# The readout of the last state moved behind the rates and the second drive in each step of a selective scan (one Trainium2 core)

## The reference, cut to what matters

```
def step(h, inp):
    d_t, u_t, B_t, C_t = inp
    dA = jnp.exp(d_t[..., None] * A)
    dBu = (d_t * u_t)[..., None] * B_t[:, None, :]
    h = dA * h + dBu
    y = jnp.einsum('bdn,bn->bd', h, C_t)
    return (h, y)
```

## Time and profile before

| what | value |
|---|---|
| median of 3 runs | 1948.91 us (1948.72 to 1953.33) |
| the profiled execution's own time | 1953.92 us |
| its span, first to last instruction | 1952.1 us |
| mean granted TensorE clock, share of full | 0.916 |
| PE busy over the span | 1711.4 us (88%) |
| state loop, from the first readout's start to the last's | 463.6 to 1043.0 us |

### The profile page before, as it was taken

One profiled execution on the slowest core, in us unless ns is written; L12 is line 12 of the kernel. 1 busy time (PEld: TensorE's weight loads), 2 busy tenths in 40 slices (PEclk: granted clock), 3 DMA queues, 4 the chain that ended last, 5 costly groups with the idle time before them and its releaser, 6 DMA issues.

```text
span 1952.1 us, 24426 instructions
## 1 busy us (share of the span) xinstructions
PE 1711.4 (88%) x9096; PEld 821.3 (42%) x9096; DVE 1011.8 (52%) x1520; ACT 761.7 (39%) x1201; POOL 703.1 (36%) x430
## 2 busy tenths in 40 slices
PE   7888886898999999999997759999812979899998
PEld 4666663542322332332333525444401557644443
DVE  2444444255888888888884333222359464522121
ACT  1333332196676666666661222111413240112121
POOL 0433330215998998998995010000000014000000
PEclk8999997798999999999999768999865879789999
DMA  2111101002000100100100600111062100101110
GB/s 68 32 32 32 32 27 52 0 8 96 12 12 7 29 12 7 29 12 7 29 6 17 223 1 0 33 48 32 5 143 70 33 0 1 44 1 43 44 43 21
DMA packets 36491, 65.63 MB, mean 34 GB/s; under 512 B 13509, under 2 KB 22617, under 8 KB 34981
## 3 DMA queue, kind: packets, MB, share of 16 engines
q1 hardware_dynamic: 33204, 63.42, 11.0%
q10 hardware_dynamic: 3200, 1.07, 0.2%
HBM read 55.80 MB, written 8.67 MB: 33 GB/s over the span
## 4 chain that ended last, share of the span: by engine, by line
PE 80%; DVE 12%; ACT 2%; DMA 2%; issue 2%; POOL 1%; SPq 1%; DVEq 0%; ACTq 0%; POOLq 0%
PE ps L845 17%; PE ps L888 7%; PE ps L1376 6%; PE ps L2123 6%; PE ps L2112 6%; PE ps L860 5%; PE ps L201 4%; PE ps L1389 3%; PE ps L342 3%; PE ps L347 3%; PE ps L224 3%; PE ps L360 2%; DVE arena L477 2%; PE ps L1887 2%; PE ps L1903 2%
## 5 line engine op out<-in xcount | busy, mean ns | idle before, releaser
L1156 POOL TENSOR_TENSOR arena<-arena 128x768 f32<-128x768 f32 x248 | 521.5, 2122 | 75.2 <-DVE arena L1106 45.0
L845 PE MATMUL ps<-arena 32*128 32x512 f32 x2016 | 368.7, 647 | 2.9 <-DMA arena<-m_bd 2.9
L1106 DVE TENSOR_TENSOR arena<-arena,ps 128x1024 f32<-128x1024 f32 x248 | 302.0, 1218 | 11.7 <-POOL arena L1156 5.5
L845 PEld LDWEIGHTS ps<-arena 32*128 32x128 f32 x2016 | 130.0, 184 | 194.2 <-issue 165.2
L1086 DVE TENSOR_TENSOR arena<-arena,ps 128x1024 f32<-128x1024 f32 x124 | 151.4, 1221 | 87.5 <-PE ps L845 87.5
L1012 ACT ACTIVATE arena<-arena 128x1024 f32<-128x1024 f32 x124 | 131.0, 1057 | 166.1 <-DVE arena L1086 166.1
L2069 POOL TENSOR_TENSOR arena<-arena 128x1024 f32<-128x1024 f32 x16 | 29.9, 1896 | 435.0 <-DVE arena L2002 421.7
L888 PE MATMUL ps<-arena 128*32 128x512 f32 (+15 forms) x1024 | 136.2, 604 | 9.4 <-DVE arena L1106 8.9
L1019 ACT ACTIVATE arena<-ps 128x1024 f32<-128x1024 f32 x124 | 127.0, 1024 | 19.7 <-PE ps L845 3.4
L1021 ACT ACTIVATE arena<-arena 128x1024 f32<-128x1024 f32 x124 | 131.1, 1057 | 3.9
L1376 PE MATMUL ps<-arena 128*128 128x512 f32 x288 | 131.8, 602 | 0.6 <-ACT arena L1441 0.6
(11 more groups left out here) (291 smaller groups left out, 2345.3 us busy)
## 6 DMA issues: line engine op xcount, KB each, us to landing
arena<-ctxT SPq DMA_DIRECT2D x32, 257.0 KB, 3.0
arena<-ctxT SPq DMA_DIRECT2D x8, 1028.0 KB, 15.2
arena<-L_ffn_w SPq DMA_DIRECT2D x16, 512.0 KB, 4.3
arena<-ctx_rows SPq DMA_DIRECT2D x8, 960.0 KB
m_rows<-arena SPq DMA_DIRECT2D x16, 256.0 KB, 3.0
arena<-m_rows SPq DMA_DIRECT2D x64, 64.0 KB
arena<-L_ffn_eW SPq DMA_DIRECT2D x8, 512.0 KB, 3.5
m_yd<-arena SPq DMA_DIRECT2D x64, 32.0 KB, 2.3
```

Source lines behind the costliest of these rows:

```text
L845: mm = nc.tensor.matmul(ps[:, bank + jj, :], weights[r], m_row[r, n // CH % 2, n % CH, :], start=start, stop=True)
L1106: nc.vector.tensor_tensor(m_h[:, u, n % 2], m_xa[:, u, n % 2], ps[:, bank:bank + 2, :], ALU.add).then_inc(S["m_use"], 1)
L1156: nc.gpsimd.tensor_tensor(x, x, m_h[:, u, (n - 1) % 2].rearrange("p j d -> p (j d)")[:, own], ALU.mult).then_inc(S["m_kept"], 1)
```

## The change

In each step of PE's program the call of `read_out(n - 1)` moves from between the drive of unit 0 and the rates to behind the drive of unit 1, ahead of the logs. The ring's order, all semaphores and the programs of all other engines stay as they are.

```diff
             logs(1)
             for n in range(STEPS):
                 drive(n, 0)
-                if n:
-                    read_out(n - 1)
                 if rated(n + 2):
                     rates(n + 2)
                 drive(n, 1)
+                if n:
+                    read_out(n - 1)
                 if rated(n + 2):
                     logs(n + 2)
             read_out(STEPS - 1)
```

## The result

The changed kernel takes 2003.24 us (median of 4 runs, 1996.8 to 2008.46) against 1948.90 before: the ratio is 1.0272, 95% interval 1.0238 to 1.0305. The forecast was 2001 us, slower. The profiled execution took 2003.58 us against 1953.92. From the first readout to the last the loop now takes 464.0 to 1091.7, 627.7 us, against 579.4: 48.3 of the 49.7 us between the two profiled executions.

A forecast was written before the change was run, and what follows sets the result against it. The prediction took a 4.57 us chain through readout, rates, DVE and unit 1's state as the bound, replaced by 5.05 through the logs. 120 x 0.48 = 57.6, less 5.6, on 1948.9 gave 2001 us, range 1988 to 2018.

The forecast's parts named there:

- What bounded the loop before: Readout, rates, DVE's reading, state of unit 1 and back to the readout set each step before the change: 4.57 us.
- PE's stream: Rival, 4%: PE's own instruction sequence bounds the loop, giving 1938 or 1949 us; against it, only 4.10 a step.
- Point 1: Rates start at once, without the readout ahead; the chain through state and rates loses 0.99 us, needing 3.58.
- Point 2: The readout in front of the logs enters the log chain: 4.06 us becomes 5.05, a step 0.48 longer.
- the log chain: One-step loop of log spread, ACT's reading, drive of unit 1, newly the readout, and log products: 4.06 us before, 5.05 after.
- The two edges without a row: Readout straight to log products and drive of unit 1 straight to readout, taken as 0.99 and 1.06 us.
- Neither bound: On those PE edges, readout costing 0.90 gives -11 us; later giving way gives up to +17: 1990 to 2018.
- Point 3: At turns without rates or logs, two readout spacings take 7.09 against 8.48: 1.39 less each, -5.6 with the loop's end.
- the two-step chain: Through unit 1's state, readout, logs, drive of unit 0 and DVE after the change: 8.74 us, or 4.37 a step.
- The sum: Over the loop, 120 spacings x 0.48 = 57.6, less 5.6 for turns and loop's end: +52.0 us.
- The faster one: Rival, 6%: the readout streams beside the drive or log products, a step takes POOL's 4.20, total about 1900 us.
- The clock: Rival, 10%: PE's longer waits lower its granted clock once per eight steps, 16 x 1.66 = 27 more: 2028 us.

The follow-up runs named there:

- experiment 2: DVE's reading of the rates (L1086) halved to 512 columns: in the changed kernel 2003.4 us (1.0263), in the kernel before 1920.4 us (0.9838).
- experiment 3: Readout cut to 256 of 512 channels: in the changed kernel 1952.0 us (1.0017), in the kernel before 1919.3 us (0.983).
- experiment 1: ACT's reading of the logs (L1019) halved to 512 columns: in the changed kernel 1952.2 us (0.9996), in the kernel before 1948.9 us (0.9974).
- experiment 4: Changed kernel with the readout moved behind the logs: 2047.1 us; or between the rates and the drive of unit 1: 1972.9 us, 4.73 a step.
- experiment 5: Logs given their own PSUM buffer, drives and rates sharing two: under the changed order 2053.4 us (1.0529), under the order before 1950.9 us (1.0002).
- experiment 6: Order before, with unit 1 ahead of the rates and logs in their own buffer: 2110.2 us; or with a third state tile, readout two steps back: 1941.2 us.

## Why the prediction was right, and where its terms were off

**What bounded the loop before: right.** The loop fell from 4.57 to POOL's pace when either of two of its links was cut (experiments 2 and 3), and did not move with ACT's reading (experiment 1). One piece of evidence was weaker than I took it for. The 120.9 us of weight load idle under L1106 are mostly the time in which the array streams: after the change 96.4 us stand under the same name, while the state had ended well ahead. What carried the argument were the starts: the readout began at 618.98, 0.06 behind the end of the state, and PE would have come free at 618.91, so the real wait was 0.07. The weight loads' busy share, which I also cited against PE's stream, does not tell the cases apart: 173.39 of 592 us (29%) before, 172.19 of 644 (27%) after, and 164.43 of 582 (28%) in the order of experiment 4 that PE's stream bounds.

**Point 1, the rates without the readout ahead: right but worth nothing.** DVE's idle before L1086 fell from 87.5 us in the page before to 21.7 in the page after, and halving the rates changed nothing under the new order.

**Point 2, the log chain: right in every link.** Forecast 1.18 + 1.02 + 0.05 + 1.06 + 0.99 + 0.75 = 5.05; measured 5.05. The two edges without a row came out as taken: drive of unit 1 to readout 641.90 to 642.96, 1.06; readout to log products 642.96 to 643.95, 0.99. Neither bound was used. Cutting ACT's reading or the readout shortened the step one for one, and a ring without that wait (experiment 5) put a state in its place, as its sum said.

**Point 3, the turns: two terms off, small.** I forecast 7.09 for the two spacings of a turn and 5.05 for the next, 12.14; measured 3.64 + 3.04 + 5.74 = 12.42. The first is 0.22 shorter than my 3.86 because two spreads on the same rows take 1.91 together and not 2.12, the second 0.19 shorter than my 3.23 for that reason (0.10) and because the drive of unit 1 starts 0.04 behind the rates and not 0.12: the two terms that experiment 4 exposed. The 0.12 stands in my sums of PE's stream (4.10) and of the two-step chain (8.74) as well, where it decided nothing. The third spacing was missed: at 613.08 the log products started 0.05 behind the end of the state of unit 0 (613.03) with PE free since 612.96, and L1019 of that step began at 615.58, 0.10 behind the end of the state of unit 1, instead of behind the log spread. At the turn the loop is bound by the states once more.

**The sum.** The loop has 127 spacings between 128 readouts. 114 ordinary ones x 0.48 = 54.7; three turns 12.42 against 8.48 + 4.55, -0.6 each, -1.8; a stretch of low clock at the third turn that only the execution before had the earlier trace rows, -1.7; the last three spacings, 3.64 + 2.05 + 4.42 against 4.56 + 3.93 + 4.26, -2.6; the first, 5.06 against 5.29, -0.2. That is +48.4, and the loop shows +48.3. I had 120 x 0.48 less 5.6, +52.0, so the loop's forecast was 3.7 too high: six spacings that I counted as ordinary are the first one, the third of each turn and two at the end. That the total came within 2 us is in part luck: the two profiled executions lie 49.7 apart and the medians 54.3, on runs that spread over 5 us before and 12 after.

**The rivals.** The faster one fell to the spacing and to experiment 3. PE's own stream does not bound the changed order, since a shorter instruction of ACT shortens it (experiment 1); it does bound the one of experiment 4, at 4.73. The rule of the Trainium skill, TensorEngine Tiling, section Key Properties, that a change of tiling mode drains TensorE was not needed: the step came out at 5.05 without it. No run here sets a change of shape apart from the rest. The clock stayed at 0.99.

Not tried: a ring of four buffers, which would free the drive of unit 1 from both waits; the loop's three buffers of two banks and the two readout banks take all eight banks that the kernel lays out in PSUM (`ps`).

## What to carry to other kernels

In a loop of engines joined by a ring of buffers, moving a product takes it out of one closed chain and puts it into another; before moving it, sum each chain that passes its new place, the buffer waits included, even those that show no wait now. A hidden chain with 0.51 us to spare cannot take 0.99 more. A releaser's name beside an idle time is a lead, not a proof: compare its end with the start of what is said to wait.

## What the hardware showed that I had not expected

- DVE's carry of 128x256, both inputs in SBUF, took 0.42 us in the steps of before, where POOL was idle when it began; 0.80 when it began 1.30 us into POOL's shorter carry (experiment 2), ending 0.28 behind that carry; and 2.20 when it began 0.45 us into POOL's longer one (experiment 6), ending 0.29 behind it. DVE's operations with one input in PSUM ran 1.22 beside POOL in all of them. The Trainium skill, SBUF — State Buffer, section Who interferes with whom, says that such an instruction and one of GpSimd that reads SBUF contend for a shared port pair, an exclusive lock, and that the order of issue decides who blocks; these traces agree where DVE comes second. POOL's pace at full load was 4.29 to 4.30 a step and not the 4.20 of its two carries back to back: in experiment 2 its longer carry took 2.55 us (2.42 before), with the end of DVE's carry in its first 0.3 us.
- Two spreads on the same rows, one behind the other, took 1.93 us together (0.98 + 0.95, experiment 4), where a single one ahead of another tile shape takes 1.06. Two on different rows started 0.01 us apart.
- A readout of half the columns costs 0.56 us and not half of 0.99.
